# Macaron block on one core: where the biases of four projections are added

## The reference, cut to what matters

```python
x = x + 0.5 * ffn(layernorm(x))
x = x + attn(layernorm(x))
x = x + 0.5 * ffn(layernorm(x))

def ffn(x):                       # H = 16 "heads" of 16 features, L = 64, E = 8 experts
    h  = rmsnorm(x, gamma1)
    q  = (h @ Wq + bq)                                  # 256 -> 256
    kv = ((h @ Wdown + bdown) @ Wup + bup)              # 256 -> 64 -> 512, split into k and v
    att = softmax(einsum('bthd,btgd->bthg', q, k) / 4)  # within a token: head against head
    out = einsum('bthg,btgd->bthd', att, v)
    x  = x + (out @ Wo + bo)                            # 256 -> 256
    h2 = rmsnorm(x, gamma2)
    gate = softmax(h2 @ Wg + bg)
    return x + sum_e gate[e] * (h2 @ We[e])             # eight 256 x 256 experts

def attn(x):                      # 8 heads of 32 features, over the 512 tokens of a batch
    q, k, v = x @ Wq + bq, x @ Wk + bk, x @ Wv + bv
    return softmax_over_heads(q k^T / 16) @ v           # the softmax runs over the 8 heads
```

## Time and profile before

| | |
|---|---|
| timed executions, us | 1225.77, 1220.3, 1222.15 (median 1222.15) |
| the profiled execution, us | 1226.44, with a span of 1224.6 from first to last instruction |
| mean granted TensorE clock | 0.962 of full speed |
| busy: TensorE matmuls | 1077.6 us, 88% of the span |
| busy: VectorE | 918.6 us, 75% |
| busy: ScalarE | 583.8 us, 48% |
| busy: GpSimd | 645.1 us, 53% |
| bias matmuls (line 394) | 144, 61.4 us busy, 427 ns mean |
| chain that ended last, by engine | TensorE 77%, VectorE 14%, nothing visible ("issue") 5%, ScalarE 3%, GpSimd 1% |

### The profile page before, as it was taken

The page is one execution under the profiler, slowest core; times in us unless marked ns, Lnnn a source line. Parts: engine busy times, 40 slices in busy tenths (PEclk is TensorE's granted clock), DMA queues, the critical chain, the costliest instruction groups (busy, mean ns, idle before and its releaser), DMA issues.

```text
span 1224.6 us, 34307 instructions
## 1 busy us (share of the span) xinstructions
PE 1077.6 (88%) x14480; PEld 818.1 (67%) x14480; DVE 918.6 (75%) x1448; ACT 583.8 (48%) x1132; POOL 645.1 (53%) x552
## 2 busy tenths in 40 slices
PE   4689999999999977887887877767799999999997
PEld 3578888878778844544554545436587888888785
DVE  6588888778784387887888878795776977977752
ACT  2445345345444455666656655532343444444442
POOL 6543564554543356666666766671344545554434
PEclk9799999999999998999999999887799999999999
DMA  6200000000000000000000000000000000000000
GB/s 193 71 3 2 2 3 2 2 3 2 3 2 1 1 1 1 1 1 1 1 1 1 1 1 1 1 1 3 3 1 20 20 2 20 18 3 20 20 2 35
DMA packets 8151, 14.40 MB, mean 12 GB/s; under 512 B 2488, under 2 KB 5822, under 8 KB 8000
## 3 DMA queue, kind: packets, MB, share of 16 engines
q1 hardware_dynamic: 8000, 12.22, 2.9%
HBM read 8.02 MB, written 4.19 MB: 10 GB/s over the span
## 4 chain that ended last, share of the span: by engine, by line
PE 77%; DVE 14%; issue 5%; ACT 3%; POOL 1%; DMA 0%; DVEq 0%; POOLq 0%; ACTq 0%
PE psum L388 45%; DVE oT L1012 9%; PE psum L535 8%; PE psum L722 5%; PE psum L710 5%; PE psum L737 4%; PE psum L394 2%; ACT kvx L1188 2%; PE psum L614 1%; PE psum L573 1%; PE psum L647 1%; PE psum L624 1%; PE psum L631 1%; DVE late L1018 1%; DVE kvx L876 1%
## 5 line engine op out<-in xcount | busy, mean ns | idle before, releaser
L388 PE MATMUL psum<-we,h 128*128 128x512 f32 x1536 | 400.1, 404 | 0.6 <-issue 0.6
L388 PEld LDWEIGHTS psum<-we,h 128*128 128x128 f32 x1536 | 278.1, 189 | 61.5 <-issue 1.5
L1284 POOL TENSOR_TENSOR late<-late 128x512 f32<-128x512 f32 x64 | 83.5, 1305 | 238.1 <-ACT late L1139 238.1
L1012 DVE TENSOR_REDUCE oT<-psum 128x256 fp32r<-128x2048 f32 x64 | 146.5, 2289 | 72.7 <-PE psum L710 72.6
L1139 ACT ACTIVATE late<-psum,gate 128x256 f32<-128x256 f32 x256 | 107.1, 470 | 169.4 <-PE psum L388 135.7
L985 DVE SCALAR_TENSOR_TENSOR X<-psum,gate,X 128x256 f32<-128x256 f32 x256 | 123.3, 482 | 77.8 <-PE psum L388 39.8
L1188 ACT ACTIVATE kvx<-psum 128x1024 f32<-128x1024 f32 x128 | 124.0, 1022 | 72.3 <-PE psum L722 72.2
L1306 POOL TENSOR_TENSOR kvx<-kvx,late 128x2048 f32<-128x2048 f32 x32 | 123.6, 3864 | 63.2 <-ACT late L1195 63.2
L1306 POOL TENSOR_TENSOR late<-kvx,late 128x2048 f32<-128x2048 f32 x32 | 123.7, 3867 | 60.7 <-ACT late L1195 60.7
L1018 DVE TENSOR_REDUCE late<-kvx 128x256 f32<-128x2048 f32 x64 | 145.7, 2276 | 0.0
L722 PE MATMUL psum<-oT,neg_id 128*128 128x512 f32 x256 | 78.8, 431 | 57.3 <-DVE oT L1012 57.3
(11 more groups left out here) (142 smaller groups left out, 1954.3 us busy)
## 6 DMA issues: line engine op xcount, KB each, us to landing
X<-in_L_attn_hidden_states SPq DMA_DIRECT2D x8, 512.0 KB, 4.7
out<-X SPq DMA_DIRECT2D x8, 512.0 KB, 2.6
X<-in_L_ffn_We SPq DMA_DIRECT2D x2, 1024.0 KB, 8.7
kvx<-in_L_ffn_Wq SPq DMA_DIRECT2D x1, 256.0 KB, 3.0
kvx<-in_L_ffn_Wup SPq DMA_DIRECT2D x2, 128.0 KB, 2.7
kvx<-in_L_ffn_Wo SPq DMA_DIRECT2D x1, 256.0 KB, 4.1
late<-in_L_attn_Wk SPq DMA_DIRECT2D x1, 256.0 KB, 10.1
late<-in_L_attn_Wq SPq DMA_DIRECT2D x1, 256.0 KB, 7.3
```

The source lines that it names most:

```text
L388: ins = e.matmul(out_ap, l, r, start=(n == 0 and not opened), stop=(n == len(terms) - 1), skip_group_check=opened)
L1012: e.tensor_reduce(mr[u % 2][:, :], all_heads(u), AX.X, ALU.max).then_inc(a_max, 1)
L1284: own.step(e.tensor_tensor(y[:, 0:2, :], y[:, 0:2, :], y[:, 2:4, :], ALU.add))
```

## The change

Four things are changed.

1. **kv.** A new tile `la_one` (66 partitions, 512 columns) holds a copy of the high part (rows 0 to 63) that GpSimd makes in a new piece `la_one`, and ones in rows 64 and 65, written once at the start. Rows 64 and 65 of the low Wup part now hold the high and low part of bup. The second matmul of a `kv` product is `la_one` by 66 rows of it. The bias matmul is gone. `kv` waits for `la_one` too.
2. **wo.** The bias matmul is gone. bo is loaded onto all 128 partitions (`b_out`), and GpSimd adds it to the whole of `x1_base` by one tensor_tensor of 128x1024, after the four instructions there.
3. **v of the attention.** The bias matmul is gone. bv is loaded onto all partitions (`b_val`), and GpSimd adds it in a new piece `v_bias` (128x512) after `v_out`. `values` waits for it.
4. **Start.** The `bias` tile holds bq only (256 columns in place of 1280). Four loads of rows and two of 128 partitions take the place of eight loads of rows. VectorE gets two more operations on two partitions, and the list scheduler gets the new steps and durations (its `wo` no longer waits for `x1_base`, but `x1` does).

```diff
@@ -96,12 +96,13 @@
+        put("POOL", 900, ("la_one", s), ("la_hi", s), ("kv", s - 1, 1))
-            put("PE", 1400, ("kv", s, p), ("la_lo", s), ("values", units - 2 * NT - 1) if s >= B else None, *((f"expand_{w}", c - 3) for w in "VPA"),
+            put("PE", 930, ("kv", s, p), ("la_lo", s), ("la_one", s), ("values", units - 2 * NT - 1) if s >= B else None, *((f"expand_{w}", c - 3) for w in "VPA"),
@@ -121,10 +122,10 @@
-        put("POOL", 2300, ("x1_base", s), ("scaled", s), ("half", s - 1), ("xs2", s - 1), ("score", units - 1) if s >= B else ("rest_lo", 10))
+        put("POOL", 4900, ("x1_base", s), ("scaled", s), ("half", s - 1), ("xs2", s - 1), ("score", units - 1) if s >= B else ("rest_lo", 10))
-            put("PE", 1650, ("wo", s, p), ("oT_lo", s, KC - 1), ("x1_base", s), ("rest_lo", 4))
-            put("DVE", 680, ("x1", s, p), ("wo", s, p))
+            put("PE", 1420, ("wo", s, p), ("oT_lo", s, KC - 1), ("rest_lo", 4))
+            put("DVE", 680, ("x1", s, p), ("wo", s, p), ("x1_base", s))
@@ -185,8 +186,9 @@
-            add("PE", 2050, ("v", b, n), ("a_hT_lo", b, KC - 1), ("values", 8 * (b - 1) - 1))
+            add("PE", 1420, ("v", b, n), ("a_hT_lo", b, KC - 1), ("values", 8 * (b - 1) - 1))
+            add("POOL", 1300, ("v_bias", b, n), ("v_out", b, n))
@@ -203,7 +205,7 @@
-            add("PE", 1000, ("values", u), ("normalise", u), ("v_out", u // 8, 1), ("a_add", u // NT - 1))
+            add("PE", 1000, ("values", u), ("normalise", u), ("v_bias", u // 8, 1), ("a_add", u // NT - 1))
@@ -333,7 +335,7 @@
-        row1 = sbt(ctx, "row1", [2, 1])
+        row1 = sbt(ctx, "row1", [HALF + 2, 1])
@@ -342,9 +344,11 @@
-        BQ, BU, BO, BV = (0, D), (D, 2 * D), (3 * D, D), (4 * D, D)
-        NB = 5 * D
-        bias = sbt(ctx, "bias", [P, NB], F32R)
+        bias = sbt(ctx, "bias", [P, D], F32R)
+        b_out = sbt(ctx, "b_out", [P, D])
+        b_val = sbt(ctx, "b_val", [P, D])
+        KVB = slice(HALF, HALF + 2)
@@ -388,11 +394,10 @@
-        def open_with_bias(e, bank, at, times):
-            lo, n = at
-            e.matmul(psum[:, bank, 0:times * n].rearrange("p (t n) -> p t n", t=times), ones2[:, :],
-                     bias[:, lo:lo + n].unsqueeze(1).to_broadcast([P, times, n]), start=True, stop=False, skip_group_check=True)
+        def open_with_bias(e, bank):
+            e.matmul(psum[:, bank, :].rearrange("p (t n) -> p t n", t=2), ones2[:, :],
+                     bias[:, :].unsqueeze(1).to_broadcast([P, 2, D]), start=True, stop=False, skip_group_check=True)
@@ -414,6 +419,7 @@
+        la_one = sb("la_one", [HALF + 2, S], F32R)
@@ -442,16 +448,17 @@
-        for n in (KC * 2 * L, KC * D, KC * D, 2 * D, NB):
+        for n in (KC * 2 * L, KC * D, KC * D, 2 * D, 2 * D):
-        raw_b = stage[0:2, ends[4]:ends[5]]
-        spare = h2[1][0:2, :, :, :].rearrange("p x k t -> p (x k t)").bitcast(F32)
-        bhi, ones2f = spare[:, 0:NB], spare[:, NB:NB + P]
+        raw_b = stage[0:2, ends[4]:ends[4] + D]
+        raw_kvb = stage[KVB, ends[4]:ends[5]]
+        spare = [h2[1][rows, :, :, :].rearrange("p x k t -> p (x k t)").bitcast(F32) for rows in (slice(0, 2), KVB)]
+        bhi, ones2f, kvbhi = spare[0][:, 0:D], spare[0][:, D:D + P], spare[1][:, 0:2 * D]
@@ -585,7 +592,7 @@
                     e.wait_ge(s_hT_lo, 2 * k + 2)
-                    open_with_bias(e, b, BQ, 2)
+                    open_with_bias(e, b)
@@ -594,11 +601,13 @@
+                        e.wait_ge(s_const, 5)
+                    e.wait_ge(s_la_one, k + 1)
-                        terms = [(la[:, i * P:(i + 1) * P], wu[:, y_, :]) for y_ in (0, 1)]
-                        open_with_bias(e, 3 + i % 2, BU, 1)
-                        ins = product(e, psum[:, 3 + i % 2, :], terms, True)
+                        terms = [(la[:, i * P:(i + 1) * P], wu[:, 0, :]),
+                                 (la_one[:, i * P:(i + 1) * P], wu[0:HALF + 2, 1, :])]
+                        ins = product(e, psum[:, 3 + i % 2, :], terms)
@@ -636,9 +645,8 @@
-                    open_with_bias(e, b, BO, 2)
-                        ins = product(e, psum[:, b, (i % 2) * D:(i % 2 + 1) * D], three(oT, i, wo), True)
+                        ins = product(e, psum[:, b, (i % 2) * D:(i % 2 + 1) * D], three(oT, i, wo))
@@ -689,9 +697,8 @@
                         e.wait_ge(s_rest, 8)
-                    open_with_bias(e, bk, BV, 2)
                     for c, i in enumerate(tiles_of[n]):
-                        ins = product(e, psum[:, bk, c * D:(c + 1) * D], three(hT, i, aw[2]), True)
+                        ins = product(e, psum[:, bk, c * D:(c + 1) * D], three(hT, i, aw[2]))
@@ -726,7 +733,7 @@
-                    e.wait_ge(a_v, 2 * b + 2)
+                    e.wait_ge(a_vb, 2 * b + 2)
@@ -788,7 +795,8 @@
-            e.tensor_copy(row1[:, :], ident[0:2, 1:2]).then_inc(s_consts_dve, 1)
+            own.step(e.tensor_copy(row1[0:2, :], ident[0:2, 1:2]))
+            e.tensor_copy(row1[KVB, :], ident[KVB, HALF + 1:HALF + 2]).then_inc(s_consts_dve, 1)
@@ -836,7 +844,13 @@
                 elif piece == ("split_lo", 3):
-                    split_lo(wu[:, 1], raw_u, wu[:, 0], l_wu, 32, 4)
+                    e.wait_ge(s_consts_dve, 2)
+                    e.wait_ge(s_hi, 3)
+                    own.step(e.tensor_scalar(kvbhi.bitcast(F32R), kvbhi, row1[KVB, 0:1], None, ALU.mult))
+                    e.wait_ge(own.sem, own.n)
+                    own.step(e.tensor_tensor(wu[KVB, 1, :], raw_kvb, kvbhi, ALU.subtract))
+                    split_lo(wu[0:HALF, 1], raw_u[0:HALF, :], wu[0:HALF, 0], l_wu, 32, 4)
@@ -1042,7 +1056,9 @@
-                    split_hi(bhi.bitcast(F32R), raw_b, l_bias, 128)
+                    e.wait_ge(l_bias, 64)
+                    e.activation(bhi.bitcast(F32R), raw_b, ACT.Copy)
+                    e.activation(kvbhi.bitcast(F32R), raw_kvb, ACT.Copy).then_inc(s_hi, 1)
@@ -1216,6 +1232,7 @@
+            e.memset(la_one[:, :].bitcast(F32), 1.0).then_inc(s_const, 1)
@@ -1233,7 +1250,7 @@
-                    own.step(e.tensor_scalar(bhi.bitcast(F32R), bhi, row1[:, 0:1], 1.0, ALU.mult, ALU.mult))
+                    own.step(e.tensor_scalar(bhi.bitcast(F32R), bhi, row1[0:2, 0:1], 1.0, ALU.mult, ALU.mult))
@@ -1273,7 +1290,12 @@
                                               ALU.mult, ALU.add)
-                    ins.then_inc(s_x1p, 1)
+                    own.step(ins)
+                    if k == 0:
+                        e.wait_ge(l_bout, 16)
+                    e.wait_ge(own.sem, own.n)
+                    e.tensor_tensor(x1[:, :, :], x1[:, :, :], b_out[:, :].unsqueeze(1).to_broadcast([P, NT, D]),
+                                    ALU.add).then_inc(s_x1p, 1)
@@ -1298,6 +1320,20 @@
                     e.tensor_tensor(a_rs[:, 2, :], a_rs[:, 2, :], a_rs[:, 0, :], ALU.mult).then_inc(a_rstd, 1)
+                elif name == "la_one":
+                    if k == 0:
+                        e.wait_ge(s_const, 5)
+                    else:
+                        e.wait_ge(s_kv, 2 * k)
+                    e.wait_ge(s_la_hi, k + 1)
+                    e.tensor_scalar(la_one[0:HALF, :], la[0:HALF, :].bitcast(F32), 1.0, 1.0, ALU.mult, ALU.mult).then_inc(s_la_one, 1)
+                elif name == "v_bias":
+                    b, n = piece[1:]
+                    rows = v[b % 2][:, tiles_of[n][0]:tiles_of[n][-1] + 1, :]
+                    if b == 0 and n == 0:
+                        e.wait_ge(l_bval, 16)
+                    e.wait_ge(a_v, 2 * b + n + 1)
+                    e.tensor_tensor(rows, rows, b_val[:, :].unsqueeze(1).to_broadcast([P, 2, D]), ALU.add).then_inc(a_vb, 1)
@@ -1321,9 +1357,9 @@
-            for (lo, n), name in ((BQ, "L0_ffn_bq"), (BU, "L0_ffn_bup"), (BO, "L0_ffn_bo"), (BV, "L0_attn_bv")):
-                for r in range(2):
-                    e.dma_start(raw_b[r:r + 1, lo:lo + n], a[name].rearrange("(o n) -> o n", o=1)).then_inc(l_bias, 16)
+            for r in range(2):
+                e.dma_start(raw_b[r:r + 1, :], a["L0_ffn_bq"].rearrange("(o n) -> o n", o=1)).then_inc(l_bias, 16)
+                e.dma_start(raw_kvb[r:r + 1, :], a["L0_ffn_bup"].rearrange("(o n) -> o n", o=1)).then_inc(l_bias, 16)
@@ -1331,6 +1367,8 @@
+            e.dma_start(b_out[:, :], a["L0_ffn_bo"].rearrange("(o n) -> o n", o=1).to_broadcast([P, D])).then_inc(l_bout, 16)
+            e.dma_start(b_val[:, :], a["L0_attn_bv"].rearrange("(o n) -> o n", o=1).to_broadcast([P, D])).then_inc(l_bval, 16)
```

4 lines of the change are left out of this document (3 added, 1 removed).

## The result

The changed kernel took 1216.53 us (median of 10 runs, 1211.30 to 1219.92) beside 1225.72 us of the kernel before on the same chip (10 runs, 1219.91 to 1229.10): ratio 0.9930, 95% interval [0.9906, 0.9954]. The change brings 0.5 to 0.7%, 6 to 9 us; the forecast was 18 us. The range 1195 to 1217 held the time, at its edge. Profiles are of one execution each: two of the changed kernel differ by 7 us at the start of the eighth job.

A forecast was written before the change was run, and what follows sets the result against it. TensorE was taken to bound the feed-forward stretches, a chain of waits the attention. 21.3 us of removed matmuls less 3 us of added pauses gave 18.3 us, so 1222.15 us becomes 1204 us; range 1195 to 1217.

The forecast's parts named there:

- the price of a matmul: In TensorE's full stream a bias matmul of 512 columns costs 0.23 us.
- the clean job: A steady feed-forward job, TensorE busy throughout, was to go from 45.7 to 44.3 us.
- the allowance for pauses, 3 us: TensorE's 22 us of pauses in the full feed-forward stretches were to grow by 3 us, about 0.2 a job.
- I count the start as 0, bounds -1 to +1: Changed bias-row loading and splitting at kernel start was to change the time by 0, between -1 and +1 us.
- My third rival: Half the gain: worse-fitting lists, unexplained pauses or low clock add 10 us of pauses, giving 1211 us; chance 0.14.
- Gross gain, 21.3 us: Removed bias matmuls: 17.9 us in the full stretches, 1.6 in the attention, 1.8 in the first 75 us.
- taken as 0: Eight matmuls removed between 815 and 875 us: worth between 0 and 1.8 us, counted as 0.
- VectorE and GpSimd together: Added GpSimd work holds VectorE up by at most 3.0 us a job: 40.1 of 44.3, still under TensorE.
- The bound I gave for the addition in `x1_base`: Addition ahead of rms1_pow and xs, with 2.0 us of cover: priced at nothing, bound 0.6 us a job.
- The new order should place it where it fits: The scheduler, told 4.9 us for x1_base against 4.4 expected, should place the addition without cost.
- The first rival: x1_base ahead of rms1_pow delays the next job's transposes, 2.2 us in 14 jobs, giving 1232 us; chance 0.06.
- the three signs of being wrong: Pauses at xs transposes or kv ending on GpSimd; products 0.4 us apart after la_one; full-stretch pauses over 22 by 10.

The follow-up runs named there:

- after_again: The changed kernel, unaltered, run again on another chip beside the kernel before: ratio 0.9948 [0.9924, 0.9972].
- same_order_again: The changed kernel's operations in the engine order lists of the kernel before, new pieces put in, repeated on one chip with the changed kernel: ratio 0.9850 [0.9813, 0.9887].
- drop_only: The kernel before with the 112 bias matmuls of kv, wo and v left out and nothing put in their place: 1195.44 us, ratio 0.9800.
- drop_again: Repeat on another chip of the kernel before without its 112 bias matmuls and nothing in their place: 1197.95 us, ratio 0.9778.
- memset_add: The changed kernel in the order lists of before, each output-bias addition replaced by eight 128x256 GpSimd memsets on an unread buffer: 1205.75 us, ratio 0.9886.
- same_order: The changed kernel, all operations kept, in the engine order lists of the kernel before with the new pieces put in: 1206.09 us, ratio 0.9868.
- late_add: The changed kernel in the order lists of before, output-bias addition moved behind the next job's rms1_pow and xs on GpSimd: 1203.36 us, ratio 0.9822.
- no_add: The changed kernel in the order lists of before, without the 16 GpSimd additions of the output projection's bias: 1200.63 us, ratio 0.9845.
- split_add: The changed kernel in the order lists of before, each output-bias addition as four 128x256 instructions instead of one 128x1024: 1204.24 us, ratio 0.9881.

## Why the prediction was wrong

The direction, the price of a matmul and the clean job were right; the sum was 18.3 us and the result 6 to 9. The profiles, cut at the start of the third down projection, the first and the last maximum of the attention, and the start of the eleventh down projection, show where (us):

| stretch | before | changed | after_again | same_order_again |
|---|---|---|---|---|
| start to third job | 94.6 | 99.1 | 100.0 | 91.2 |
| third job to attention | 330.4 | 323.7 | 329.8 | 325.2 |
| attention | 381.6 | 384.9 | 378.5 | 379.2 |
| attention to eleventh job | 90.0 | 77.1 | 77.4 | 78.1 |
| the rest | 328.0 | 326.2 | 328.2 | 327.6 |

The gain of the fourth row, 11 to 14 us, came in every variant (drop_only 77.3); the forecast had at most 1.8 there.

- *The step that failed is the allowance for pauses, 3 us, and with it "I count the start as 0, bounds -1 to +1": together they price the new order of the lists at next to nothing.* The 3 us stood for "jobs become 3% shorter with unchanged latencies". What the runs showed in its place is the new lists, 8 to 12 us: no latency but another order. The start was to become 1.8 us shorter and became 4.5 to 5.3 longer, and the held operation at unit 55 cost 3 us in an attention that was to lose 1.6. In the full stretches TensorE's pauses grew from 22 us to 25.8 and 29.3, and some jobs ran at a lower clock (51.2 us at 0.93). Ten jobs there (third to eighth down projection and eleventh to sixteenth) took 467.9 us before, 463.3 and 471.6 in the two profiles of the changed kernel, 462.0 in drop_only; the clean job alone would have brought them 12 us. So 3 us was too little even for drop_only, which has neither new work nor new lists (6 us of 11 came), and far too little for the new lists. My third rival, "half the gain", named this ("The new lists fit worse") and priced it, pauses and low clock together, at 10 us; against the gross gain of 21.3 it came to 13 to 15. It was the right case with 0.14 of the chance.
- *Gross gain, 21.3 us: probably too small.* drop_only and drop_again measured 24 and 27. The 0.23 us each held. The sum names only 104 of the 112 matmuls (78 + 14 + 4 + 8): six before 75 us and two just before 815 us are given nothing without a word, and eight of the 104 were "taken as 0". All 112 at 0.23 give 25.8. The profiles point at the filling as well: from the last maximum to the first expert product the kernel before took 72.3 us, drop_only 60.9, and all the other variants 58.8 to 62.5. TensorE's waits there (806 to 880 us), before:

```profile
PE psum L535 <- issue: 7.8, 4, 2.3
```

  In drop_only this row is 0.4 us, once, between 796 and 870 us. These are the pauses without a visible owner that the earlier trace rows showed: 24.3 us in 15 before, 16.3 to 21.1 in the four profiles with the new lists, 11.1 to 17.7 in all others. Whether they went because matmuls did, or the one profile of before was unlucky, was not settled.
- *"VectorE and GpSimd together ... as a bound of its own it would add nothing here" was wrong in its reasoning.* I compared busy sums: 40.1 of 44.3 us, "still under TensorE". But an operation that is held is held at one place, and in the lists of before VectorE was behind TensorE's list there, with 1.4 us of cover for 2.2 us of delay. The average over the job says nothing on that place. With 0.76 us in a job the additions cost 6 us in those lists. The bound I gave for the addition in `x1_base`, 0.6 us a job, was of the right size. In the changed kernel itself this step decided little as far as the trace shows: TensorE waits 1.2 us for it. "The new order should place it where it fits" came true in the clean job, by luck: nothing in the planner knows that VectorE stands still meanwhile, and the start and unit 55 got what the clean job was spared.
- *The first rival* described this very place, with x1_base ahead of `rms1_pow`. Its mechanism, VectorE waiting for the power, is in the trace of memset_add, but its path is not: the transposes of `xs` wait for GpSimd 14.2 us in 2 in the changed kernel, as they did before (13.7 in 2). Its price of 2.2 us a job ignored the cover on VectorE and TensorE.
- *The clock is a term that the sum did not have.* The mean granted clock of the timed runs is 0.958 in the changed kernel, 0.967 in the kernel before beside it (chip of after_again), 0.961 and 0.963 in the two same_order runs and 0.965 in late_add. Over all timed runs, 0.001 less within one kernel goes with 0.76 us more. By that, my estimate, some 6 to 7 us between the kernel before and the changed one, and 2 to 4 of the 8 to 12 us of the lists, come with a lower clock. Its low stretches are the start (0.84 in the changed kernel's first 99 us, 0.89 in the first 95 us before), the attention and the filling. Whether the clock fell because the new lists have pauses there, or would have fallen anyway, no run parts.

With the lists of before the same change brought 16 to 18 us, close to the 18.3 forecast. That is luck: the matmuls brought 3 to 6 us more than I said, and the additions took about 6 of which I said nothing.

Of the signs named ahead, a job of 44.3 us (44.5), 32 matmuls, 0.23 us between the products and 1.9 to 2.6 us for the addition (2.38) came true; none of the three signs of being wrong appeared, though the forecast was wrong: the start had no sign, and the pauses in the full stretches were to exceed 22 us by more than 10 and did by 4 and 7. As forecast, `la_one` and the additions to the values cost nothing that can be measured. In the attention the unit that carries the second bias of a batch became 0.24 us shorter in each batch (0.23 forecast). The low part of the bias rows became 1.2 us long instead of 2.88, and nothing was gained at the start.

The Trainium skill, "SBUF — State Buffer", section "Who interferes with whom", says that the two engines share one port pair which one of them holds for a whole instruction. With this the trace agrees: 2.38 us behind 2.39, 0.76 at most behind quarters, 0.30 at most behind memsets of 0.30. The page ties the lock to VectorE's instructions that use the shared port. The trace agrees that not all are held: the two at 34.14 and 34.84 us, which read PSUM, ran beside 9.15 us of GpSimd.

## What to carry to other kernels

Before work goes to GpSimd, look up in the timeline which short VectorE operation will run beside it and who waits for that one: one long GpSimd instruction beside or ahead of what leads to the freeing of a PSUM bank costs what the cover there lacks, whatever the busy shares say. A kernel whose order is planned has a second change in each change: run the edit in the old order first (here 16 to 18 us), and then judge the new order by itself (minus 8 to 12). Name a sign of being wrong for every stretch, the start too. Variants are compared on one chip: no_add looked 5 us slower than drop_only on two chips and was within 3 us of it on one.

## What was not expected of the hardware

- A 128x1024 tensor_tensor on GpSimd with one input repeated takes 2.38 us; on the line through the 128x512 and 128x2048 rows it was 2.16.
- Some of VectorE's operations on four columns last as long as what is left of the GpSimd instruction beside them: 3.08, 3.11 and 4.42 us for 0.17.
- A 66-row product of 512 columns costs a stream 0.23 us, as with 128 rows.
- A wait shorter than the cover is free, and two causes at one place hide each other: shortening the holding alone (memset_add, split_add) brought nothing.
